# Gate and up projections as Strassen block products, with weights unpacked once and streamed over four sweeps

## The reference

```python
Wg = dequant_nvfp4(gate_W_packed, gate_scales)     # [4096, 512], likewise Wu; Wd is [512, 4096]
gate = jnp.einsum('th,nh->tn', xt, Wg)             # xt: 4096 tokens x 512
up = jnp.einsum('th,nh->tn', xt, Wu)
gelu = jnp.tanh(0.7978845608028654 * (gate + 0.044715 * gate ** 3)) * gate * 0.5 + gate * 0.5
inter = gelu * up
out = jnp.einsum('tn,hn->th', inter, Wd)           # then x = layernorm(x + out)
```

## Time and profile before

| | us |
|---|---|
| three runs | 3125.22, 3125.49, 3128.05 (median 3125.49) |
| span of the profiled execution (its own time, the edges of a run left out) | 3122.8 |
| PE busy in the span | 2909.1 |
| DVE, ACT, POOL busy | 1996.8, 1248.3, 942.4 |
| attention part, to about | 920 |
| feed-forward matmuls | 942.1 to 3093.4 |

### The profile page before, as it was taken

One profiled execution on the slowest core, in us unless ns is written; L12 is line 12 of the kernel. 1 busy time (PEld: TensorE's weight loads), 2 busy tenths in 40 slices (PEclk: granted clock), 3 DMA queues, 4 the chain that ended last, 5 costly groups with the idle time before them and its releaser, 6 DMA issues.

```text
span 3122.8 us, 47560 instructions
## 1 busy us (share of the span) xinstructions
PE 2909.1 (93%) x14080; PEld 2436.7 (78%) x14080; DVE 1996.8 (64%) x4200; ACT 1248.3 (40%) x2869; POOL 942.4 (30%) x1041
## 2 busy tenths in 40 slices
PE   4999999989958999999999999689999999999996
PEld 4888778878836888888888888568888888888885
DVE  3887778778865566655666556545666556666565
ACT  3877777777732222222222322122222222222221
POOL 1443334334322232222232222322222222322223
PEclk9999999999978999999999999889999999999998
DMA  5566565656545000000000000150000000000001
GB/s 173 149 170 175 160 178 140 183 161 177 140 124 182 21 28 27 21 27 20 27 25 22 27 20 27 57 193 21 28 26 21 27 20 27 24 23 27 20 27 54
DMA packets 156540, 234.00 MB, mean 75 GB/s; under 512 B 10488, under 2 KB 77176, under 8 KB 156408
## 3 DMA queue, kind: packets, MB, share of 16 engines
q1 hardware_dynamic: 156408, 232.63, 25.8%
HBM read 165.48 MB, written 67.11 MB: 74 GB/s over the span
## 4 chain that ended last, share of the span: by engine, by line
PE 65%; SPq 1%; DMA 1%; DVE 1%; POOL 1%; issue 1%; ACT 0%; POOLq 0%; DVEq 0%; ACTq 0%
PE bank L849 22%; PE bank L850 22%; PE bank L851 22%; DMA scale<-gate_scales 1%; POOL acc L1045 1%; SPq L799 1%; SPq L804 0%; DMA bx_l<-x1T_scratch 0%; DVE bstats L1009 0%; SPq L812 0%; DVE w L966 0%; SPq L816 0%; DVE bmean_var L1012 0%; DVE bits_a L961 0%; DVE bits_b L953 0%
## 5 line engine op out<-in xcount | busy, mean ns | idle before, releaser
L1035 POOL TENSOR_TENSOR inter_l<-hid,inter_h 128x512 fp32r<-128x512 f32 x256 | 347.3, 1357 | 1207.9 <-ACT inter_h L916 1207.9
L984 DVE SCALAR_TENSOR_TENSOR hid<-hid,bank 128x512 f32<-128x512 f32 x256 | 176.0, 687 | 777.6 <-ACT hid L909 777.6
L849 PE MATMUL bank<-bx_h,wg_h 128*128 128x512 f32 x1024 | 402.3, 393 | 85.3 <-DMA bx_l<-x1T_scratch 68.3
L684 POOL TENSOR_SCALAR probs<-probs,row_inv 128x128 f32<-128x128 f32 (+3 forms) x512 | 264.5, 537 | 540.4 <-DVE row_inv L603 540.4
L850 PE MATMUL bank<-bx_l,wg_h 128*128 128x512 f32 x1024 | 401.2, 392 | 0.0
L851 PE MATMUL bank<-bx_h,wg_l 128*128 128x512 f32 x1024 | 400.8, 391 | 0.0
L849 PE MATMUL bank<-wd_h,inter_h 128*128 128x512 f32 x1024 | 398.6, 389 | 0.5 <-DVE acc L976 0.5
L851 PE MATMUL bank<-bx_h,wu_l 128*128 128x512 f32 x1024 | 398.4, 389 | 0.0
L850 PE MATMUL bank<-bx_l,wu_h 128*128 128x512 f32 x1024 | 398.4, 389 | 0.0
L850 PE MATMUL bank<-wd_l,inter_h 128*128 128x512 f32 x1024 | 398.4, 389 | 0.0
L851 PE MATMUL bank<-wd_h,inter_l 128*128 128x512 f32 x1024 | 398.3, 389 | 0.0
(11 more groups left out here) (96 smaller groups left out, 5561.1 us busy)
## 6 DMA issues: line engine op xcount, KB each, us to landing
qk_scratch<-qk_stage SPq DMA_DIRECT2D x64, 512.0 KB, 2.9
q_st<-qk_scratch SPq DMA_DIRECT2D x128, 256.0 KB, 5.1
k_st<-qk_scratch SPq DMA_DIRECT2D x128, 256.0 KB, 7.0
x1T_scratch<-x_stage SPq DMA_DIRECT2D x64, 256.0 KB, 3.7
codes<-gate SPq DMA_DIRECT2D x33, 256.0 KB
scale<-gate_scales SPq DMA_DIRECT2D x66, 128.0 KB
codes<-up SPq DMA_DIRECT2D x33, 256.0 KB
scale<-up_scales SPq DMA_DIRECT2D x66, 128.0 KB
```

The costliest lines, as they stand in the source:

```text
L684: pool.tensor_scalar(p, p, row_inv[:, h % 4, k:k + 1], 1.0, ALU.mult, ALU.mult).then_inc(norm_done, 1)
L849: pe.matmul(out, at(a[0]), bt(b[0]), start=(c == 0), stop=False)
L984: dve.scalar_tensor_tensor(h, h, 1.0, g_bank[m][:, :], ALU.add, ALU.mult).then_inc(poly_done, 1)
L1035: pool.tensor_tensor(inter[1][:, j % 2, m, :], hid[:, m, :], f32(inter[0][:, j % 2, m, :]), ALU.subtract).then_inc(inter_split, 1)
```

## The change

**Strassen's products.** Four old quarter-results, 2 feature halves m x 2 token tiles t, with K split in two halves of 256, are now computed together as a *quad*: one group of 256 features with 1024 tokens. Seven products (the Winograd variant) of sums and differences of blocks replace eight: for gate and up each 7 products x 2 K-chunks x 3 = 42 matmuls of 512 columns. `down` is unchanged in size: 8 pieces of 6 matmuls for a quad. The weight sums (4 of 7 blocks) are made by POOL before the split, the x sums by DVE. The results are combined in PSUM: ACT copies product 1 from bank A to bank B (`seed`), further products are accumulated on it; partial sums u2, u3 are copied out by ACT (`take_u2`, `take_u3`), DVE makes C22 (`make_c22`) and writes a starting value into bank E (`seed_e`). Six PSUM banks serve gate and up, two serve down.

**Sweeps.** The tokens go in four sweeps of 1024 with 16 quads each, 64 quads `j`, written out without loops. In the first sweep (`prep`) all three units of the next quad are unpacked within each quad, split, and stored to `w_scratch` in DRAM. In the other sweeps `load_w` streams the split weights (4.72 MB per quad, 14,336 and 8,192 bytes for a partition) one quad ahead.

**x.** `x1T_scratch` has one plane, unsplit: ACT copies one half of a transposed tile, DVE the other. In the last quad of a sweep (`last`) the next sweep's x is loaded, summed by DVE (`sum_x`), copied by ACT (`x_part`, 1024 columns each, seven blocks), and subtracted by POOL (`x_low`); at the start DVE does the subtraction.

**Ends.** Statistics are split by token tile and placed in the next sweep's first quads; the root is a power on POOL and a Newton step on DVE; POOL normalises into a staging buffer that is stored, and `acc` is loaded again.

The core of the diff:

```diff
@@ attention, ACT and DVE @@
-                            copy(x1_stage[:, t % 2, 0, :].bitcast(F32R), t_bank[t % 2][:, :]).then_inc(t_high, 1)
+                            copy(x1_stage[:, t % 2, 0:256], t_bank[t % 2][:, 0:256]).then_inc(t_high, 1)
...
-                            low(x1_stage[:, t % 2, 1, :].bitcast(F32R), t_bank[t % 2][:, :],
-                                x1_stage[:, t % 2, 0, :]).then_inc(t_free, 1)
+                            dve.tensor_copy(x1_stage[:, t % 2, 256:], t_bank[t % 2][:, 256:]).then_inc(t_free, 1)
@@ SP @@
+            for j in range(QUADS):
+                st, first = j // NG, j % NG == 0
+                if j + 1 < NG:
+                    for u in range(UNITS):
+                        k = UNITS * (j + 1) + u
+                        if k + 1 < UNITS * NG:
+                            load_unit(k + 1)
+                        if u:
+                            store_w(j + 1, u - 1)
+                    store_w(j + 1, 2)
+                elif j + 1 < QUADS:
+                    sp.wait_ge(prod_done, 14 * j)
+                    load_w(j + 1, 0)
+                    load_w(j + 1, 1)
+                if first and st:
+                    store_out(st - 1, 0)
+                    store_out(st - 1, 1)
...
+                    load_x(st + 1, x_next)
+                if NG <= j + 1 < QUADS:
+                    sp.wait_ge(down_done, 8 * j)
+                    load_w(j + 1, 2)
@@ TensorE @@
+            def down(j, n):
...
+                if 8 * j + n >= 2:
+                    pe.wait_ge(d_added, 8 * j + n - 1)
...
+            for j in range(QUADS):
+                p1(j, "g")
+                p1(j, "u")
+                down(j - 1, 0)
+                p6(j, "g")
+                p2(j, "g")
+                p6(j, "u")
+                p2(j, "u")
+                down(j - 1, 1)
+                down(j - 1, 2)
+                p7(j, "g")
+                p5(j, "g")
+                down(j - 1, 3)
+                p7(j, "u")
+                p5(j, "u")
+                down(j - 1, 4)
+                p4(j, "g")
+                p4(j, "u")
+                down(j - 1, 5)
+                p3(j, "g")
+                p3(j, "u")
+                down(j - 1, 6)
+                down(j - 1, 7)
@@ ACT @@
+                seed(j, "g")
+                seed(j, "u")
+                take_u2(j, "g")
+                split_high(j - 1, 1, 1)
+                square(j, 0, 0)
+                take_u2(j, "u")
+                split_high(j - 1, 0, 1)
+                tanh(j, 0, 0)
+                if prep:
+                    gate_up_high(j + 1, 0)
+                take_u3(j, "g")
+                split_high(j, 0, 0)
+                take_u3(j, "u")
+                square(j, 1, 1)
+                tanh(j, 1, 1)
+                if prep:
+                    sums_high(j + 1, 0)
+                if last:
+                    x_part(st + 1, 0, x_next)
+                    x_part(st + 1, 1, x_next)
+                if prep:
+                    gate_up_high(j + 1, 1)
+                square(j, 1, 0)
...
+                tanh(j, 1, 0)
+                if prep:
+                    sums_high(j + 1, 1)
+                split_high(j, 1, 0)
+                square(j, 0, 1)
...
+                tanh(j, 0, 1)
...
+                if prep:
+                    down_high(j + 1)
@@ DVE @@
+            def unpack_scale(k):
+                dve.wait_ge(bit_step, 5 * (k + 1))
+                if k:
+                    dve.wait_ge(w_split, k)
...
+                add_down(j - 1, 0)
+                poly(j, 0, 0)
+                gelu(j, 0, 0)
+                times_up(j, 0, 0)
...
+                if prep:
+                    unpack_bits(k)
+                add_down(j - 1, 1)
+                add_down(j - 1, 2)
+                if prep:
+                    unpack_scale(k)
+                make_c22(j, "g")
+                seed_e(j, "g")
+                add_down(j - 1, 3)
...
+                poly(j, 1, 1)
+                make_c22(j, "u")
+                seed_e(j, "u")
+                gelu(j, 1, 1)
+                times_up(j, 1, 1)
...
+                if prep:
+                    unpack_bits(k + 1)
+                add_down(j - 1, 4)
+                if prep:
+                    unpack_scale(k + 1)
+                if last:
+                    sum_x(st + 1, x_next)
+                poly(j, 1, 0)
+                gelu(j, 1, 0)
+                times_up(j, 1, 0)
+                add_down(j - 1, 5)
+                if prep:
+                    unpack_bits(k + 2)
+                poly(j, 0, 1)
+                gelu(j, 0, 1)
+                times_up(j, 0, 1)
+                if prep:
+                    unpack_scale(k + 2)
+                add_down(j - 1, 6)
+                add_down(j - 1, 7)
@@ POOL @@
+                split_low(j - 1, 1, 1)
+                split_low(j - 1, 0, 1)
...
+                if prep:
+                    sum_w(j + 1, 0)
+                split_low(j, 0, 0)
...
+                if prep:
+                    gate_up_low(j + 1, 0)
+                    sum_w(j + 1, 1)
...
+                if last:
+                    for i in range(5):
+                        x_low(st + 1, i)
+                if prep:
+                    gate_up_low(j + 1, 1)
+                split_low(j, 1, 0)
...
+                if prep:
+                    down_low(j + 1)
```

More of the change, by code:

```diff
@@ L699 @@
 TILE = 512
[L700 to L702 removed]
+SWEEP = 2 * TILE
+NS = TOK // SWEEP
 SUB = TILE // P
@@ L864, in down @@
-            def down(step, w, parity):
-                pe.wait_ge(inter_split, step * 2 + (2 + SPLIT_CREDIT))
-                for q in range(SUB):
-                    pe.wait_ge(d_added, step * SUB + (q + 1))
-                    for m in range(2):
-                        last = three(d_bank[q][:, :], inter, wd, m, 2,
-                                     lambda x: x[:, parity, m, q * P:(q + 1) * P],
-                                     lambda x: x[:, w, m, :])
-                    last.then_inc(d_done, 1)
@@ L924, in tail, with copy, x_part @@
-            def tail(st):
-                act.wait_ge(var_done, st + 1)
-                act.activation(std[:, :], var_eps[:, :], ACT.Sqrt).then_inc(std_done, 1)
-            steps(act, tail, body)
+            def copy(out, in_):
+                return act.activation(out, in_, ACT.Copy)
+            def x_part(st, i, stage):
+                act.wait_ge(x_loaded, 64 * (st + 1))
+                if i in (1, 3, 4, 5):
+                    act.wait_ge(x_summed, 4 * (st + 1))
+                if st:
+                    act.wait_ge(prod_done, product(NG * st - 1, "u", {v: k for k, v in B_SLOT.items()}[i]))
+                copy(x_h[:, i, :, :], stage[:, i, :, :]).then_inc(x_high, 1)
@@ new lines, in tanh, with split_high @@
+            def tanh(j, m, t):
+                h = hid[:, 2 * m + t, :]
+                act.wait_ge(poly_done, chain(j, m, t))
+                act.activation(h, h, ACT.Tanh, scale=C1).then_inc(tanh_done, 1)
+            def split_high(j, m, t):
+                if j < 0:
+                    return
+                act.wait_ge(hid_done, chain(j, m, t))
+                if j:
+                    act.wait_ge(down_done, down_at(j - 1, t, 3))
+                copy(inter[0][:, m, t, :], hid[:, 2 * m + t, :]).then_inc(inter_high, 1)
@@ L1002, in tail, with add_down @@
-            def tail(st):
-                for j in (STEPS - 2, STEPS - 1):
-                    for q in range(SUB):
-                        add_down(st * STEPS + j, j % ST, q)
-                n = SUPER // P
-                dve.wait_ge(d_added, (st + 1) * (STEPS * SUB) + ADD_CREDIT)
-                for a in range(n):
+            def add_down(j, n):
+                if j < 0:
+                    return
+                if j % NG == 0 and n % 4 == 0:
+                    dve.wait_ge(acc_loaded[n // 4], 16 * (j // NG + 1))
+                dve.wait_ge(down_done, 8 * j + n + 1)
+                a = acc[:, n, :]
+                dve.tensor_tensor(a, a, d_bank[n % 2][:, :], ALU.add).then_inc(d_added, 1)
@@ L1054, in program @@
+            split_low(QUADS - 1, 1, 1)
+            split_low(QUADS - 1, 0, 1)
+            for t in range(2):
+                root(NS - 1, t)
+            for t in range(2):
+                normalise(NS - 1, t)
 def program(nc, a, out):
```

629 lines of the change are left out of this document (413 added, 216 removed).

## The result

The changed kernel takes 3213.7 us (median of 4 runs, 3208.5 to 3218.6) against 3126.8 us for the kernel before in the same job: 1.028 times as long, with a 95% interval of 1.026 to 1.030. The span of the profiled execution is 3206.5 us; forecast were 3220 and, as a time, 3222.

What follows compares the result with a forecast made beforehand. It took TensorE as the feed-forward bound before, and a DVE-POOL-ACT chain in the new first sweep; unpacking costs about 250 us against 174 + 36 gained, giving 3222 us, range 3085 to 3310.

Steps and rivals of the forecast that it cites:

- Matmuls gone, 174 us: All 64 quads: 132 matmuls replace 144, 29.9 us a quad, saving 174 us if TensorE never waits.
- rivals 3 and 4: Weight stream bounds sweeps 2 to 4: 3404 us, chance 0.07; accumulating or loopless code costs TensorE every quad: 3270, 0.05.
- The first sweep, 48.5 us a quad: Quads with unpacking inside: chain through fixed engine orders and three units gives period 48.5 us, bounds 32 and 59.
- Rival 1: First sweep: POOL and DVE interleave in small pieces, unpacking better covered, period 40, 3100 us; chance 0.23.
- Quad 0, 41.5 us: First quad of the first sweep, without adds or downs: period 41.5 us.
- The signs: First sweep: TensorE near 62%, DVE over 75%, 132 matmuls in 48.5 us, L956 and L953 well over 1 us, downs waiting.
- The clock, 2 us a quad: First sweep, behind down 0: TensorE restarts at the lower clock after its pause, adding 2 us to the chain.
- Rival 2: Sweep 1: clock stays low, TensorE becomes the bound at some 58 us, 3358 us; chance 0.08.
- Mutual exclusion: First sweep: certain DVE operations and POOL ones exclude each other; period 48.5 us with it, 40 without.
- Changes of sweep, 14 us each: Three x changes: late x 8 us, clock 2, weights behind the store 4; 42 us together, bounds 0 and 80.
- Start and attention: Attention saves 6 us (bounds 0 and 15); second part's start brings quad 0's unpack_scale at 981 before that saving.
- The sum: Whole kernel: quad 15 ends at 1710, plus 1434.5, 42 and 33: span 3220 us, time 3222, 3% slower.

Runs made afterwards that it cites:

- e4: Changed kernel with only quads 0 and 1 unpacked; quads 2 to 63 load one of these two's stored weights, mostly wrong ones; 2966.6 us.
- e1: Changed kernel with DVE's add 6 right behind add 5 and add 7 right behind the last bit operations in the first sweep; 3213.4 us.
- e7: Changed kernel with adds 6, 7 and chain (0,1) earlier, down_high later, sweep changes reordered, further moves on ACT, DVE and at the start; 3077.3 us.
- e3: Changed kernel with the weights' low parts (gate_up_low, down_low) computed by DVE instead of POOL; 3175.5 us.
- e6: Changed kernel with x loaded before the weights, sum_x earlier, fewer x_low ahead of split_low, and a sweep's second store behind the weights' loads; 3172.1 us.
- e2: e1 plus ACT's down_high moved into the next quad, behind square(0,0); 3168.5 us.

## Why the prediction was right, step by step

- **Matmuls gone, 174 us:** right. 29.9 us a quad in e4 and in the later sweeps, no wait in the steady quads, and no cost of streaming or of the code without loops (rivals 3 and 4 are out).
- **The first sweep, 48.5 us a quad:** right in mechanism, 0.7 us too long. Each third of the chain was within 1.8 us of the trace. The walk left out two locked-out operations (poly and times_up of (1,1), 1.6 us more, in the first third), and had 1.1 us too much in the second third. So part of the closeness is errors that cancel. As a claim of what *sets* it, it was too narrow: it named add 6 and down 0, and e1 shows that ACT's down_high, standing ahead of the seeds, holds the same spot. Rival 1 had 40; e7 came near it (40.8) only by reordering.
- **Quad 0, 41.5 us:** wrong. Its scalings run from 960.9 to 1008.0, 47.1 us: without adds and downs the chain through the three units is nearly as long. The thirteen quads after it took 619.7 us instead of 630.5 and hid this in the sum.
- **The signs:** 132 matmuls a quad, L1169 and L1172 above 1 us, and the waits of `down` for `acc` came as said. TensorE was busy 76% instead of near 62%, since its matmuls at the lower clock count for longer (0.63 us instead of 0.39), and DVE 73 to 74% instead of over 75%.
- **The clock, 2 us a quad:** the trace has 11 matmuls from 1230.64 on at 0.43 us between starts instead of 0.23, 2.2 us, behind a pause of 4.2 us. No run takes it away; that it adds to the period in full is argued from the chain. Rival 2 is out: the mean in the sweep was 0.86 and not the bound.
- **Mutual exclusion:** shown by e3. The rule of the Trainium skill ("SBUF — State Buffer", SBUF: two separate sides), that a DVE operation with two SBUF inputs and a POOL one hold each other off for a whole instruction, agrees with the trace: L1227 on `u3` 1596 ns beside POOL, 693 without. It named more operations than my rows did. For sum_x the sum took nothing for it (5.3 us), and the sentence beside it 2.6 us; the three sum_x took 7.0, 6.5 and 6.5 us, one subtraction of each lengthened beside POOL's x_low, so the sum was 1 to 2 us short there. For `u3` I missed it.

```profile
1684.56 3.35 DVE L1150 TENSOR_TENSOR x_next<-x_next 128x1024 f32<-128x1024 f32 x1
```

- **Changes of sweep, 14 us each:** right in mechanism, 15.7, 15.3 and 15.6 in the trace, counted as what the four quads around each take above 29.9 a quad; e6, which undoes the queues named and moves sum_x forward, removed 42 us.
- **Start and attention, the part that was off:** the second part began 15.3 us earlier (first SP issue at 905.2, before 920.5), not 6. About 10 of it stands before the last normalisation of attention (DVE at 894.2, before 904.4), at the upper part of my bounds. The other 5 is the hand-over behind it: the transposed x is half as large and was stored sooner; I had counted this at nothing. Not all of the 15.3 is the change's: in the seven other traces, whose attention code is the same, the second part begins at 907.1 to 912.4, and of the kernel before there is one trace only. The start then took 55.7 us to quad 0's first unpack_scale instead of 60.5; 3 us of this because x came by 917.6, 12 us after the first issue, not 16.
- **The sum:** counted at TensorE's first matmul of quad 16 (1700.2 us) and of the last downs (3172.9), it was 9 us too late at the start of the second part, 5 in the start, 6 in quads 0 to 15; 6 too early in the later sweeps, 1 in the tail: before rounding 13.5 us on 3206.5. Errors of both signs make it up, so it is closer than its parts. The profiled execution is the fastest of four; against their median the forecast time is 8 us too long.

## What to carry to other kernels

When a change puts more work for helper engines into a unit of the bound engine's time, add up not their busy time but one full turn of the chain through their fixed orders: here every helper was busy for under 75% of the quad, and the quad was still 60% longer. Moving one holder of a chain can give nothing while a second stands at the same spot (e1), and both together gave 45 us (e2), until a third showed. Before using POOL beside DVE, list DVE's operations with no input in a PSUM bank: here some with both inputs in SBUF and the one-input bit operations were held where they met a POOL operation, and those with an input in a bank were not (L1198, L1213, L1218, L1227: 683 to 688 ns).

## What the runs showed of the hardware

A locked-out DVE operation can take four times its length: L1169 took 2.75 us once in every quad of the first sweep instead of 0.69, beside a POOL subtraction of 2.56 us. DVE's three bit operations with one input, L1166, L1172 and L1174 (0.42 to 0.43 us with POOL idle), are not spared: 738, 1076 and 759 ns on the average. POOL pays as well: its subtraction of 256 columns (L1348) took 723 ns at its shortest and 1183 on the average for the gate weights.

The length of a pause does not tell alone whether TensorE's clock falls. In the kernel after, between quads 1 and 15, the first matmul behind 14 of 16 pauses of 3.3 to 3.4 us took 0.50 us, so the clock was high; behind 26 of 27 pauses of 3.9 to 5.3 us it took 0.76 to 0.80. In e1 all 14 pauses of 3.39 to 3.43 us were followed by the lower clock, and in e7 8 of 14 pauses of 2.81 to 2.85 us.
